# Cross-attention and ternary FFN on one core: the tanh of the weights kept as 16-bit integers and cast by a GpSimd DMA, the output product moved ahead of the token transposes, the artanh series split

## The chip, the cores and the metric

The kernel runs on one core of one Trainium2 chip. The metric is the device time of one execution in microseconds (us), the median over several runs. Lower is better. The profile gives times from the first instruction to the last, the span; the time of an execution also holds a little outside the span.

## The reference, cut to what matters

`x` is 8 batches of 256 tokens of width 256, float32. There are two residual blocks:

```python
x = x + xattn(layernorm(x), ctx_512, Wq, Wkv_expand, Wout)   # 16 heads, 64 keys, causal mask
x = x + ffn(layernorm(x), w1, g1, w2, g2, w3, g3)            # hidden width 1024

def ternary_quant(w):
    s = mean(abs(w))
    return round(tanh(w / (s + 1e-8))) * arctanh(s)          # round(tanh) is -1, 0 or 1
def linear_bit(x, w, g):
    xq = act_quant(rmsnorm(x, g))                            # 8-bit steps per token
    return einsum('bsd,od->bso', xq, ternary_quant(w))
ffn = linear_bit(silu(linear_bit(x, w1, g1)) * linear_bit(x, w2, g2), w3, g3)
```

So each of the three 1024 x 256 weights needs one mean, one tanh with rounding, and one artanh of the mean.

## The kernel before, in words

All instructions are written out by hand, one program for each engine, and the engines meet at counting semaphores. An engine runs its program strictly in order: an instruction that waits holds up everything behind it on that engine. A batch has TB = 2 tiles of 128 tokens.

**Attention, and the front of the FFN, by batch.** Each engine has a function `iteration(j)`, called for j = 0 or 1 to 6, with batch 7 and the FFN's start written out behind it. Iteration j works on several batches at once, so that the engines have work of different stages:

- PE: `scores(j+1)`, the probability transposes `probs_T(j, 0)`, `tokens_T(j-3)` (transposes of the quantised tokens), `project(j-1)` (the output product with `woutT`, L576), `probs_T(j, 1)`, `query(j+2)`, `weigh(j)`, the mask of batch j+2, `recip_T(j)`.
- ACT (from L822): `recip_T_copy(j-1)`, `quantise(j-3)` (L806), `recip_widen(j)`, `probs_T_copy(j, 0)`, `tokens_T_copy(j-3)`, `exponentials(j+1, 0)`, `probs_T_copy(j, 1)`, `exponentials(j+1, 1)`, and last `query_copy(j+2)` (L746), on which the next iteration's `scores` wait.
- DVE (from L1070): `sums(j)` (L972), `divide(j-1)`, two `maximum(j+1, .)`, `shift(j+1, 0)`, `residual(j-1)` (L986, waits for `project`), `shift(j+1, 1)` (L965, waits for the transposes `probs_T(j, 1)` to have read the old probabilities), then `measure_sum`, `token_max(j-2)`, `aggregate_sum`, `centre(j-1)` and `token_recip(j-2)` (L1044) for the FFN's front.
- POOL (from L439): `token_scale(j-3)` (L421, waits for `token_recip`, and `quantise` waits for it), `values(j)`, `factor(j-2)`, `keys(j+2)` (L337, waits until `scores(j+1)` are done), `scaled(j-2)` (L430, waits for `quantise`), `half_sums(j+1)` (L398, on which `sums(j+1)` of DVE waits).

**The weights.** ACT sums absolute values (L774). A matmul adds them over partitions, `weight_scales` (L1098) makes the means `w_s` and `w_inv`. `weight_tanh(i)` (L781) writes tanh as float32 over `w_in`, in place, and `ternary(i)` (L991) rounds it on DVE by adding and subtracting 1.5 * 2^23, with bf16 output into `wT`. ACT calls `weight_tanh(0)` ahead of `recip_widen(2)`, `weight_tanh(1)` behind iteration 3 and `weight_tanh(2)` behind iteration 4; DVE calls the three `ternary` behind its iterations 3, 4 and 5. PE waits for all three before its first up product. The artanh of the three means is computed on POOL, a series for small means (`arctanh_terms`, L373, between iterations 1 and 2) and a logarithm for others (`log_branch`, L385, between iterations 3 and 4). The Ln itself is one small ACT instruction (L868) between `query_copy(4)` and iteration 3; its function is in another table than Exp, so an ACT_TABLE_LOAD stands before it and another before the next Exp.

**The FFN, by tile of 128 tokens.** `schedule(slot)` runs 16 tiles in slots: two up products, Silu, the gate product on DVE, the maximum for the quantisation, the quantised hidden tile `q_h` (int16) transposed by a DMA from SP, a cast on DVE, and the down product. `q_h` is first written in slot 1, long after attention's iterations.

Of the kernel before, what the change touches and what calls it, by code (L numbers as in the profile page):

```python
# [21 lines left out]
ALU = mybir.AluOpType  # L22
ACT = mybir.ActivationFunctionType
# [20 lines left out]
def build_program(nc, x_d, xT_d, ctxT_d, wqT_d, wkvT_d, woutT_d, w1T_d, g1_d, w2T_d, g2_d, w3T_d, g3_d, out_d):  # L44
# [17 lines left out]
    with stack:  # L62
        def sb(name, shape, dt=fp32):
            return stack.enter_context(nc.sbuf_tensor(name, shape, dt))
# [4 lines left out]
        def sem(name):  # L69
            return stack.enter_context(nc.semaphore(name))  # L70
# [72 lines left out]
        abs_done, wsum_done, ws_ready, small_ready, inv_step, inv_ready = map(sem, (  # L143
            "abs_done", "wsum_done", "ws_ready", "small_ready", "inv_step", "inv_ready"))
        ln_in, ln_out, ath_steps, ath_ready = map(sem, ("ln_in", "ln_out", "ath_steps", "ath_ready"))
        tanh_ready, tern_ready = sem("tanh_ready"), sem("tern_ready")

        AHEAD = 6

# [47 lines left out]
        q_h = sb("q_h", [P, 2, H], i16)  # L197
        hT_raw = sb("hT_raw", [P, 2, HC, P], i16)
        hT = sb("hT", [P, 2, HC, P], bf16)
        q_last = probs  # L200
        hT_last = half_sum[:].rearrange("p t n k -> p (t n k)").bitcast(bf16).rearrange("p (t n k) -> p t n k", t=2, k=P)
        y = sb("y", [P, 2, D])
# [45 lines left out]
        with nc.Block() as block:  # L248
# [45 lines left out]
            def _(pool):  # L294
# [71 lines left out]
                def step(instruction):  # L366
                    ath_step[0] += 1
                    instruction.then_inc(ath_steps, 1)
                    pool.wait_ge(ath_steps, ath_step[0])

                sq, poly, log, diff = (w_tmp[:, n, :] for n in range(4))

                def arctanh_terms():  # L373

                    pool.wait_ge(ws_ready, 1)
                    step(g.tensor_scalar(w_ln[:, 0, :], w_s[:], 1.0, None, ALU.add))
                    g.tensor_scalar(w_ln[:, 1, :], w_s[:], -1.0, 1.0, ALU.mult, ALU.add).then_inc(ln_in, 1)
                    step(g.tensor_tensor(out=sq, in0=w_s[:], in1=w_s[:], op=ALU.mult))
                    step(g.tensor_scalar(poly, sq, 2.0 / 13, 2.0 / 11, ALU.mult, ALU.add))
                    for n in (9, 7, 5, 3, 1):  # L380
                        step(g.tensor_tensor(out=poly, in0=poly, in1=sq, op=ALU.mult))
                        step(g.tensor_scalar(poly, poly, 2.0 / n, None, ALU.add))
                    step(g.tensor_tensor(out=poly, in0=poly, in1=w_s[:], op=ALU.mult))

                def log_branch():  # L385

# [52 lines left out]
                def iteration(j):  # L439
                    if from_(j, 3):  # L440
                        token_scale(j - 3)
                    if from_(j, 1):
                        values(j)
                    if from_(j, 2):
                        factor(j - 2)
                    if live(j + 2):
                        keys(j + 2)
                    if from_(j, 2):
                        scaled(j - 2)
                    if live(j + 1):  # L450
                        half_sums(j + 1)

# [33 lines left out]
                pool.wait_ge(v_set, 4)  # L486
                pool.wait_ge(g_ld, 48)
                iteration(1)
                arctanh_terms()
                iteration(2)  # L490
                iteration(3)
                log_branch()
                for j in range(4, B - 1):
                    iteration(j)
                token_scale(4)
                values(7)
# [7 lines left out]
            def _(pe):  # L504
# [130 lines left out]
                def iteration(j):  # L635
                    if live(j + 1):
                        scores(j + 1)
                    if j == 0:
                        pe.wait_ge(v_set, 2)
                    probs_T(j, 0)  # L640
                    if j == 0:
                        values_of(6, bank5)
                    if from_(j, 3):
                        need(pe, rT_ready, j)
                        tokens_T(j - 3, bank5)
                    if from_(j, 1):
                        project(j - 1)
                    probs_T(j, 1)
                    if j == 0:
                        pe.wait_ge(v_set, 4)  # L650
                    if from_(j, 3):
                        need(pe, xqT_ready, j - 2)
                    if live(j + 2):
                        query(j + 2)
                    if j == 1:
                        weight_sum()
                        pe.wait_ge(ws_ready, 1)
                    weigh(j)
                    if live(j + 2):
                        mask(j + 2)  # L660
                    recip_T(j)
# [4 lines left out]
                iteration(1)  # L666
                for j in range(2, B - 1):
                    iteration(j)
                pe.wait_ge(tern_ready, 3)

                def xqT_cols(T, n):

# [70 lines left out]
            def _(act):  # L743
# [37 lines left out]
                def weight_tanh(i):  # L781


                    a.activation(w_in[:, bass.ds(i * WN, WN)], w_in[:, bass.ds(i * WN, WN)], ACT.Tanh,
                                 scale=w_inv[:, bass.ds(i, 1)]).then_inc(tanh_ready, 1)


# [34 lines left out]
                def iteration(j):  # L822
                    if from_(j, 2):
                        recip_T_copy(j - 1)
                    if from_(j, 3):
                        quantise(j - 3)
                    recip_widen(j)
                    probs_T_copy(j, 0)
                    if from_(j, 3):
                        tokens_T_copy(j - 3, bank5)  # L830
                    if live(j + 1):
                        exponentials(j + 1, 0)
                    probs_T_copy(j, 1)
                    if live(j + 1):
                        exponentials(j + 1, 1)
                    if live(j + 2):
                        query_copy(j + 2)
# [17 lines left out]
                exponentials(2, 1)  # L855
                query_copy(3)
                recip_T_copy(1)
                act.wait_ge(inv_ready, 1)
                weight_tanh(0)
                recip_widen(2)  # L860
                probs_T_copy(2, 0)
                act.wait_ge(rstd_done, 4)
# [1 line left out]
                probs_T_copy(2, 1)  # L864
                exponentials(3, 1)
                query_copy(4)
                act.wait_ge(ln_in, 1)
                a.activation(w_ln[:], w_ln[:], ACT.Ln).then_inc(ln_out, 1)  # L868
                iteration(3)
                weight_tanh(1)  # L870
                iteration(4)
                weight_tanh(2)
                iteration(5)


                def silu(T, t, b):
# [59 lines left out]
            def _(dve):  # L936
# [51 lines left out]
                    cols = bass.ds(b * BD, BD)  # L988
                    v.tensor_tensor(x_sb[:, cols], bank4[:], x_sb[:, cols], ALU.add).then_inc(bank4_free, 1)

                def ternary(i):  # L991
                    need(dve, tanh_ready, i + 1)
                    v.tensor_scalar(wT[:, i * WN:(i + 1) * WN], w_in[:, i * WN:(i + 1) * WN],
                                    ROUND, ROUND, ALU.add, ALU.subtract).then_inc(tern_ready, 1)

                dve.wait_ge(ident_set, 1)
                v.tensor_copy(ident_h[:], ident[:]).then_inc(cast_set, 1)
                dve.wait_ge(const_set, 3)
# [110 lines left out]
                for b in (3, 4):  # L1109
                    measure(b)  # L1110
                    aggregate(b)
                sums(0)
                maximum(1, 0)
                maximum(1, 1)
                shift(1, 0)
                shift(1, 1)
                for b in range(5, B):
                    measure(b)
                    aggregate(b)
                iteration(1)  # L1120
                iteration(2)
                iteration(3)
                ternary(0)
                iteration(4)
                ternary(1)
                iteration(5)
                ternary(2)
                dve.wait_ge(w_down_ready, 2)
                dequant(0, 4)
                iteration(6)  # L1130
# [159 lines left out]
```

## Time and profile before

| | us |
|---|---|
| median of 3 runs | 202.84 (201.66 to 203.04) |
| the profiled execution, its own time | 202.36 |
| its span | 200.6 |
| outside the span (202.36 - 200.6) | 1.8 |
| busy: DVE, PE, ACT, POOL | 164.4, 148.5, 142.9, 130.0 |
| mean granted TensorE clock, share of full speed | 0.903 |

Busy time is the union of an engine's instructions. A row of the timeline gives start, duration, engine, line, operation, output and input, and in square brackets the engine's idle time before it with the instruction that ended it. "<-issue" means that nothing in the profile ended that idle time.

### The profile page before, as it was taken

How to read it: one execution, taken by the hardware profiler on the slowest of the kernel's cores; microseconds unless marked ns; L12 is line 12 of the kernel's file. 1: busy time of each engine (PE TensorE's matmuls, PEld its weight loads, DVE VectorE, ACT ScalarE, POOL GpSimd, SP SyncE). 2: the span in 40 equal slices, each digit the busy share in tenths (PEclk: the TensorE clock that was granted, in tenths of full speed). 3: DMA queues.
4: the chain of work that ended last, by engine and by line, in shares of the span. 5: the costliest groups of instructions: out<-in, count | busy, mean ns of one | idle time of the engine just before them, and what ended most of it. 6: DMA issues, size and time to landing. Idle time of an engine off the chain costs nothing.

```text
span 200.6 us, 3287 instructions
## 1 busy us (share of the span) xinstructions
PE 148.5 (74%) x1082; PEld 97.3 (49%) x1082; DVE 164.4 (82%) x309; ACT 142.9 (71%) x195; POOL 130.0 (65%) x212
## 2 busy tenths in 40 slices
PE   5979886888779499697789764284888778775380
PEld 5567655676566377475557341131353243332360
DVE  1179799999788947999959598985989999999950
ACT  2026978985699586895769976696799998896220
POOL 4063727279885883877625669879878988997100
PEclk9999999999969958999699998557699999999588
DMA  5999920000000000000000000220234635534311
GB/s 167 320 379 423 400 117 0 7 0 0 3 2 0 3 0 0 3 0 0 0 3 2 0 0 0 52 52 5 52 80 88 149 82 115 120 78 100 83 54 54
DMA packets 20944, 15.02 MB, mean 75 GB/s; under 512 B 15296, under 2 KB 19648, under 8 KB 20416
## 3 DMA queue, kind: packets, MB, share of 16 engines
q1 hardware_dynamic: 20704, 14.42, 24.9%
q10 hardware_dynamic: 224, 0.39, 0.6%
q8 instruction: 9, 0.15, 0.3%
q14 instruction: 7, 0.06, 0.1%
HBM read 9.04 MB, written 2.10 MB: 56 GB/s over the span
## 4 chain that ended last, share of the span: by engine, by line
DVE 41%; POOL 15%; ACT 14%; PE 14%; issue 12%; DMA 2%; DVEq 0%; POOLq 0%; ACTq 0%
DVE c_max L1160 7%; DVE hh L1136 7%; ACT q_x L812 5%; ACT probs L769 4%; POOL u L434 4%; DVE u_max L1041 4%; PE bank L580 3%; POOL half_sum L404 3%; DVE hT L1147 3%; DVE row_max L962 3%; DVE y L1187 3%; DVE row_sum L975 2%; ACT probsT L754 2%; PE wide L587 2%; DMA out<-y 2%
## 5 line engine op out<-in xcount | busy, mean ns | idle before, releaser
L685 PE MATMUL wide<-wT,xqT 128*128 128x512 bf16 x128 | 36.0, 428 | 7.9 <-DVE hh L1136 6.7
L456 POOL TENSOR_TENSOR c_h<-hh,g3b 128x1024 f32<-128x1024 f32 x15 | 35.4, 2361 | 3.4 <-DVE hh L1136 3.3
L404 POOL TENSOR_TENSOR half_sum<-probs 128x512 f32<-128x512 f32 x16 | 20.3, 1270 | 24.9 <-ACT probs L769 24.9
L685 PEld LDWEIGHTS wide<-wT,xqT 128*128 128x128 bf16 x128 | 12.7, 107 | 25.8 <-issue 9.5
L705 PE MATMUL bank<-wT,hT 128*128 128x256 bf16 x112 | 15.9, 289 | 10.4 <-DVE hT L1147 10.4
L580 PE MATMUL bank<-woutT,attnT 128*128 128x256 f32 x64 | 20.0, 466 | 4.2 <-DVE attnT L983 4.2
L885 ACT ACTIVATE sq_junk<-hh,root_x 128x1024 bf16<-128x1024 f32 x16 | 18.3, 1147 | 5.3 <-DVE hh L1136 4.6
L769 ACT ACTIVATE probs<-probs,ln_rstd 128x1024 f32<-128x1024 f32 x16 | 18.4, 1152 | 4.9 <-DVE probs L968 4.8
L812 ACT ACTIVATE q_x<-u,round_c,qs_x 128x256 f32<-128x256 f32 x32 | 16.6, 588 | 7.1 <-issue 3.6
L434 POOL TENSOR_TENSOR u<-xc,g 128x512 f32<-128x512 f32 x16 | 20.0, 1272 | 2.4 <-ACT q_x L812 2.4
L968 DVE TENSOR_TENSOR probs<-wide,row_max 128x1024 f32<-128x1024 f32 x16 | 19.3, 1217 | 1.7 <-PE bank L506 1.6
L892 ACT ACTIVATE q_h<-c_h,qs_h 128x1024 int16<-128x1024 f32 x14 | 16.1, 1146 | 5.8 <-DVE qs_h L1174 5.8
L754 ACT COPY probsT<-bank 128x512 f32<-128x512 f32 x32 | 17.1, 584 | 3.9 <-PE bank L506 3.9
L962 DVE TENSOR_REDUCE row_max<-wide 128x16 f32<-128x1024 f32 x16 | 18.7, 1210 | 1.3 <-PE wide L540 1.3
L1136 DVE TENSOR_TENSOR hh<-gate,wide 128x1024 f32<-128x1024 f32 x16 | 19.4, 1210 | 0.1
L1160 DVE TENSOR_REDUCE c_max<-c_h 128x1 f32<-128x1024 f32 x16 | 19.3, 1208 | 0.0
L705 PEld LDWEIGHTS bank<-wT,hT 128*128 128x128 bf16 x112 | 10.6, 103 | 17.2 <-DVE hT L1147 15.7
L506 PE MATMUL bank<-ident,probs 128*128 128x128 f32 x128 | 17.8, 284 | 1.2 <-ACT probsT L754 1.2
L580 PEld LDWEIGHTS bank<-woutT,attnT 128*128 128x128 f32 x64 | 14.5, 239 | 7.6 <-DVE attnT L983 5.4
L879 ACT ACTIVATE gate<-wide,dq_x 128x1024 f32<-128x1024 f32 x16 | 17.6, 1100 | 0.0
L506 PEld LDWEIGHTS bank<-ident,probs 128*128 128x128 f32 x128 | 15.1, 147 | 3.8 <-issue 2.1
L521 PE MATMUL bank<-xT,wqT 128*128 128x256 f32 x64 | 15.4, 384 | 0.0
(122 smaller groups left out, 303.3 us busy)
## 6 DMA issues: line engine op xcount, KB each, us to landing
out<-y SPq DMA_DIRECT2D x16, 128.0 KB, 2.0
x_sb<-in_x SPq DMA_DIRECT2D x1, 1280.0 KB, 10.3
xT<-in_xT SPq DMA_DIRECT2D x1, 1280.0 KB, 17.5
w_in<-in_w1T SPq DMA_DIRECT2D x1, 1024.0 KB, 12.3
w_in<-in_w2T SPq DMA_DIRECT2D x1, 1024.0 KB, 11.4
w_in<-in_w3T SPq DMA_DIRECT2D x1, 1024.0 KB, 13.5
x_sb<-in_x SPq DMA_DIRECT2D x1, 512.0 KB, 6.4
xT<-in_xT SPq DMA_DIRECT2D x1, 512.0 KB, 7.2
```

The source lines that it names most:

```text
L404: last = g.tensor_tensor(out=half_sum[:, t, :, :], in0=e[:, :, 0, :], in1=e[:, :, 1, :], op=ALU.add)
L434: last = g.tensor_tensor(out=u[:, t, :, :], in0=xc[:, t, :].unsqueeze(1).to_broadcast([P, 2, D]), in1=g12[:], op=ALU.mult)
L456: g.tensor_tensor(out=c_h[:, t, :], in0=hh[:, t, :], in1=g3b[:], op=ALU.mult).then_inc(c_ready, 1)
L506: return nc.tensor.matmul(out, in_, ident[0:n, 0:n], is_transpose=True, start=True, stop=True)
L580: last = nc.tensor.matmul(bank4[:, t * D:(t + 1) * D], attnT[:, c, t * P:(t + 1) * P], woutT[:, c, :], start=(c == 0), stop=(c == DC - 1))
L685: last = nc.tensor.matmul(wide[:, (w * 2 + n) * 512:(w * 2 + n + 1) * 512], xqT_cols(T, w * DC + c), w_cols[:, c, n * 512:(n + 1) * 512], ...
L705: last = nc.tensor.matmul(down_banks[t][:, 0:D], (hT if T < LAST else hT_last)[:, t, n, :], wT[:, 2 * WN + n * D:2 * WN + (n + 1) * D], st ...
L769: a.activation(probs[:, t, :], probs[:, t, :], ACT.Exp, scale=ln_rstd[:, bass.ds(2 * b + t, 1)]).then_inc(probs_ready, 1)
L812: last = a.activation(q_x[:, t, w, :], u[:, t, w, :], ACT.Identity, scale=qs_x[:, t, w:w + 1], bias=round_c[:, 0:1])
L962: v.tensor_reduce(out=by_pair(row_max[:, t, :]), in_=by_head(wide, t), op=ALU.max, axis=AX.X).then_inc(max_ready, 1)
L1136: v.tensor_tensor(hh[:, t, :], gate[:, t, :], wide[:, H:2 * H], ALU.mult).then_inc(hh_ready, 1)
L1160: v.tensor_reduce(out=c_max[:, t:t + 1], in_=c_h[:, t, :], op=ALU.max, axis=AX.X, apply_absolute_value=True).then_inc(cm_ready, 1)
```

## The change

Five edits:

1. PE: `project(j-1)` goes ahead of `tokens_T(j-3)`; both keep their waits.
2. ACT: `weight_tanh(i)` writes int16 (the conversion rounds) into `tern`, a view of the tile `q_h`, and there is one such buffer: `weight_tanh(1)` and `weight_tanh(2)` wait until the DMA of the one before has landed. The three calls move to iterations 3, 4 and 5, behind `recip_T_copy(j-1)` and ahead of `quantise(j-3)`.
3. POOL: `ternary(i)` is now a DMA issued from GpSimd, `tern` (int16) to `wT` (bf16), in iteration i + 4 between `keys` and `scaled`. The three DVE instructions go. PE waits for all three DMAs.
4. POOL and ACT: the artanh series is cut in two pieces, in iterations 2 and 3 behind `scaled`, and `log_branch` goes into iteration 4 between `scaled` and `half_sums`. The Ln on ACT goes ahead of `recip_widen(2)`, where `weight_tanh(0)` was.
5. DVE: `sums(0)` goes behind the two `maximum(1, .)`.

```diff
@@ POOL
-                def arctanh_terms():
+                def log_inputs():
                     pool.wait_ge(ws_ready, 1)
                     step(g.tensor_scalar(w_ln[:, 0, :], w_s[:], 1.0, None, ALU.add))
                     g.tensor_scalar(w_ln[:, 1, :], w_s[:], -1.0, 1.0, ALU.mult, ALU.add).then_inc(ln_in, 1)
                     step(g.tensor_tensor(out=sq, in0=w_s[:], in1=w_s[:], op=ALU.mult))
-                    step(g.tensor_scalar(poly, sq, 2.0 / 13, 2.0 / 11, ALU.mult, ALU.add))
-                    for n in (9, 7, 5, 3, 1):
+
+                def series(terms):
+                    for n in terms:
+                        if n == 11:
+                            step(g.tensor_scalar(poly, sq, 2.0 / 13, 2.0 / 11, ALU.mult, ALU.add))
+                            continue
                         step(g.tensor_tensor(out=poly, in0=poly, in1=sq, op=ALU.mult))
                         step(g.tensor_scalar(poly, poly, 2.0 / n, None, ALU.add))
-                    step(g.tensor_tensor(out=poly, in0=poly, in1=w_s[:], op=ALU.mult))
+                        if n == 1:
+                            step(g.tensor_tensor(out=poly, in0=poly, in1=w_s[:], op=ALU.mult))
+
+                def ternary(i):
+                    need(pool, tanh_ready, i + 1)
+                    g.dma_start(wT[:, i * WN:(i + 1) * WN], tern).then_inc(tern_ready[i], 16)
...
                     if live(j + 2):
                         keys(j + 2)
+                    if 0 <= j - 4 < 3:
+                        ternary(j - 4)
                     if from_(j, 2):
                         scaled(j - 2)
+                    if j == 2:
+                        series((11, 9, 7, 5))
+                    if j == 3:
+                        series((3, 1))
+                    if j == 4:
+                        log_branch()
                     if live(j + 1):
                         half_sums(j + 1)
...
                 iteration(1)
-                arctanh_terms()
-                iteration(2)
-                iteration(3)
-                log_branch()
-                for j in range(4, B - 1):
+                log_inputs()
+                for j in range(2, B - 1):
                     iteration(j)
@@ PE
+                    if from_(j, 1):
+                        project(j - 1)
                     if from_(j, 3):
                         need(pe, rT_ready, j)
                         tokens_T(j - 3, bank5)
-                    if from_(j, 1):
-                        project(j - 1)
...
-                pe.wait_ge(tern_ready, 3)
+                for i in range(3):
+                    pe.wait_ge(tern_ready[i], 16)
@@ ACT
                 def weight_tanh(i):
-                    a.activation(w_in[:, bass.ds(i * WN, WN)], w_in[:, bass.ds(i * WN, WN)], ACT.Tanh,
+                    if i > 0:
+                        act.wait_ge(tern_ready[i - 1], 16)
+                    a.activation(tern, w_in[:, bass.ds(i * WN, WN)], ACT.Tanh,
                                  scale=w_inv[:, bass.ds(i, 1)]).then_inc(tanh_ready, 1)
...
                     if from_(j, 2):
                         recip_T_copy(j - 1)
+                    if 0 <= j - 3 < 3:
+                        weight_tanh(j - 3)
                     if from_(j, 3):
                         quantise(j - 3)
...
-                act.wait_ge(inv_ready, 1)
-                weight_tanh(0)
+                act.wait_ge(ln_in, 1)
+                a.activation(w_ln[:], w_ln[:], ACT.Ln).then_inc(ln_out, 1)
                 recip_widen(2)
...
-                act.wait_ge(ln_in, 1)
-                a.activation(w_ln[:], w_ln[:], ACT.Ln).then_inc(ln_out, 1)
-                iteration(3)
-                weight_tanh(1)
-                iteration(4)
-                weight_tanh(2)
-                iteration(5)
+                act.wait_ge(inv_ready, 1)
+                for j in range(3, B - 2):
+                    iteration(j)
@@ DVE
-                def ternary(i):
-                    need(dve, tanh_ready, i + 1)
-                    v.tensor_scalar(wT[:, i * WN:(i + 1) * WN], w_in[:, i * WN:(i + 1) * WN],
-                                    ROUND, ROUND, ALU.add, ALU.subtract).then_inc(tern_ready, 1)
...
-                sums(0)
                 maximum(1, 0)
                 maximum(1, 1)
+                sums(0)
...
-                iteration(3)
-                ternary(0)
-                iteration(4)
-                ternary(1)
-                iteration(5)
-                ternary(2)
+                for j in range(1, B - 2):
+                    iteration(j)
```

## Rows read from the trace of the kernel before

**Rows 1.** The page, part 1: busy us (share of the span) xinstructions of each engine
```profile
PE 148.5 (74%) x1082; PEld 97.3 (49%) x1082; DVE 164.4 (82%) x309; ACT 142.9 (71%) x195; POOL 130.0 (65%) x212
```

**Rows 2.** Windows: length, busy of PE, PEld, DVE, ACT, POOL, clock, DMA share, GB/s
```profile
66.70:82.20 15.50, 12.30 (x99) 9.49 (x98) 11.48 (x19) 10.78 (x16) 10.02 (x18) 0.78 0.00 0
82.20:95.20 13.00, 10.00 (x101) 7.43 (x99) 12.54 (x23) 9.59 (x16) 10.20 (x17) 1.00 0.00 1
...
148.00:189.00 41.00, 28.73 (x160) 13.91 (x159) 40.12 (x74) 34.05 (x42) 32.88 (x43) 0.96 0.44 97
```

**Rows 3.** Timeline of DVE, iterations 2 to 5
```profile
51.20 1.22 DVE L1041 TENSOR_REDUCE u_max<-u 128x4 f32<-128x1024 f32 x1 [1.36 <-POOL u L434]
...
65.56 0.17 DVE L1047 RECIPROCAL rm_x<-u_max 128x4 f32<-128x4 f32 x1
...
75.19 0.69 DVE L989 TENSOR_TENSOR x_sb<-bank,x_sb 128x512 f32<-128x512 f32 x1 [2.91 <-PE bank L580]
76.89 1.23 DVE L968 TENSOR_TENSOR probs<-wide,row_max 128x1024 f32<-128x1024 f32 x1 [1.00 <-PE bank L506]
...
80.97 0.16 DVE L1047 RECIPROCAL rm_x<-u_max 128x4 f32<-128x4 f32 x1
81.06 1.19 DVE L993 TENSOR_SCALAR wT<-w_in 128x2048 bf16<-128x2048 f32 x1
...
88.33 1.23 DVE L968 TENSOR_TENSOR probs<-wide,row_max 128x1024 f32<-128x1024 f32 x1
```

**Rows 4.** Timeline of ACT, from the end of iteration 2 into iteration 4
```profile
59.42 1.28 ACT L769 ACT_TABLE_LOAD   x1
...
63.76 0.58 ACT L749 COPY qT<-bank 128x512 f32<-128x512 f32 x1
64.23 2.02 ACT L784 ACTIVATE w_in<-w_in,w_inv 128x2048 f32<-128x2048 f32 x1
...
68.90 2.07 ACT L812 ACTIVATE q_x<-u,round_c,qs_x 128x256 f32<-128x256 f32 x4 [2.18 <-issue]
...
71.38 1.05 ACT L754 COPY probsT<-bank 128x512 f32<-128x512 f32 x2
```

**Rows 5.** Timeline of POOL, iterations 4 and 5
```profile
65.18 0.25 POOL L389 TENSOR_TENSOR w_tmp<-w_ln 128x3 f32<-128x3 f32 x1
...
68.19 0.62 POOL L427 TENSOR_SCALAR qs_x<-rm_x,fb_bound 128x2 f32<-128x2 f32 x2
...
70.85 0.61 POOL L340 TENSOR_TENSOR k_pair<-kT,half_of 128x256 f32<-128x256 f32 x1
71.42 2.49 POOL L434 TENSOR_TENSOR u<-xc,g 128x512 f32<-128x512 f32 x2
...
81.24 1.46 POOL L427 TENSOR_SCALAR qs_x<-rm_x,fb_bound 128x2 f32<-128x2 f32 x2 [0.60 <-DVE rm_x L1047]
```

**Rows 6.** Timeline of PE, iteration 4
```profile
65.05 1.17 PE L540 MATMUL wide<-k_pair,qT 32*128 32x128 f32 x32
66.15 1.09 PE L506 MATMUL bank<-ident,probs 128*128 128x128 f32 x8
...
71.43 3.73 PE L580 MATMUL bank<-woutT,attnT 128*128 128x256 f32 x8
74.95 1.80 PE L506 MATMUL bank<-ident,probs 128*128 128x128 f32 x8
```

**Rows 7.** DMA view: GB/s by 40th of the span; issues, KB each, us to landing
```profile
GB/s 167 320 379 423 400 117 0 7 0 0 3 2 0 3 0 0 3 0 0 0 3 2 0 0 0 52 52 5 52 80 88 149 82 115 120 78 100 83 54 54
...
out<-y SPq DMA_DIRECT2D x16, 128.0 KB, 2.0
...
x_sb<-in_x SPq DMA_DIRECT2D x1, 512.0 KB, 6.4
```

**Rows 8.** The page, part 5: half sums (busy, mean ns, idle before them)
```profile
L404 POOL TENSOR_TENSOR half_sum<-probs 128x512 f32<-128x512 f32 x16 | 20.3, 1270 | 24.9 <-ACT probs L769 24.9
```

**Rows 9.** Timeline of DVE, the start of attention
```profile
22.28 1.22 DVE L975 TENSOR_REDUCE row_sum<-half_sum 128x32 f32<-128x1024 f32 x1 [1.19 <-POOL half_sum L404]
```

More of the change, by code:

```diff
@@ L145, in build_program @@
         ln_in, ln_out, ath_steps, ath_ready = map(sem, ("ln_in", "ln_out", "ath_steps", "ath_ready"))
-        tanh_ready, tern_ready = sem("tanh_ready"), sem("tern_ready")
+        tanh_ready = sem("tanh_ready")
+        tern_ready = [sem(f"tern{i}_ready") for i in (1, 2, 3)]
         AHEAD = 6
@@ L199, in build_program @@
         hT = sb("hT", [P, 2, HC, P], bf16)
+        tern = q_h[:].rearrange("p t n -> p (t n)")
         q_last = probs
@@ L1119, in _ @@
                     aggregate(b)
-                iteration(1)
-                iteration(2)
-                iteration(3)
-                ternary(0)
-                iteration(4)
-                ternary(1)
-                iteration(5)
-                ternary(2)
+                for j in range(1, B - 2):
+                    iteration(j)
                 dve.wait_ge(w_down_ready, 2)
```

## Prediction, made blind

> **What bounds the kernel now.** I read the page first. DVE is the busiest engine, 164.4 us of 200.6, and no engine is full over the whole span [rows 1]. The windows then divide the span. From 148 to 189 us, in the FFN's slots, DVE works 40.12 us of 41.00 [rows 2]: there the end moves only if the start of the slots moves, since the change takes nothing out of them. So the change must pay in the iterations ahead of them. There an iteration with no long stall takes 13.0 us, with DVE busy 12.54 (iteration 5), and one with a stall 15.5 us (iteration 4) [rows 2]. The timelines tell what the stall is. In iteration 4 DVE waits 2.91 us for `project` (the release of L989) and 1.00 us for the transposes `probs_T(4, 1)` ahead of the second `shift` [rows 3]. PE runs `project(3)` only at 71.43, because `tokens_T(1)` stands ahead of it and waits for `quantise(1)`; and it runs it in 3.73 us at a window clock of 0.78 [rows 2, 6]. ACT begins `quantise(1)` at 68.90 after 2.18 us of idle time, since POOL comes to `token_scale(1)` only at 68.19, behind the log branch that began at 65.18 [rows 4, 5].
>
> So there is one loop over engines that sets an iteration: `token_recip` on DVE, `token_scale` on POOL, `quantise` and the copies on ACT, `probs_T(j, 1)` on PE, the second `shift` on DVE, and again to `token_recip`. I measure everything against it. From the end of `rm_x` to the start of the second `shift` it is 76.89 - 65.73 = 11.2 us in iteration 4 and 88.33 - 81.13 = 7.2 us in iteration 5 [rows 3]; the second is DVE's own work, the 1.1 us of a `ternary` in it.
>
> **What the new wait does.** `weight_tanh(1)` stands at the head of ACT's iteration 4 and waits until the DMA of `ternary(0)` has landed. POOL issues that DMA in its own iteration 4, behind `token_scale(1)`, `values`, `factor` and `keys(6)`. `keys(6)` waits for `scores(5)`, and these wait for `query_copy(5)`, ACT's last instruction of iteration 3. So POOL can't issue early: from the end of that copy ACT must wait at least for scores 1.17 [rows 6], keys 0.61 [rows 5] and the DMA, and it can only do `recip_T_copy(3)` meanwhile. Behind the waiting tanh stand `quantise`, `recip_widen`, the copies and the exponentials, so PE's token transposes and `probs_T(4, 1)`, and DVE's second `shift`, wait as well. The same happens in iteration 5. In iteration 3 the tanh has nothing to wait for, and the third DMA has nobody waiting on ACT; PE wants it only at the first up product.
>
> Price of the DMA, issue to landing: no row has a DMA issued by GpSimd, nor one that casts. It moves 128 x 2048 int16, 512 KB. The nearest rows are the stores, 128 KB in 2.0 us, and the load of 512 KB, 6.4 us beside other loads [rows 7]. I take the store, 384 KB more at the best rate seen, 423 GB/s, 0.9 us [rows 7], and 0.6 us for POOL's part: 3.5 us, between 2.0 and 6.4. How long POOL itself is held by the issue no row shows: between nothing and the 2.49 us of its longest piece of work here [rows 5]; I keep it at the 0.6.
>
> The Trainium skill (DMA: Bandwidth & Descriptors, "Anatomy of one DMA — SWDGE (gpsimd) path") gives about 2.0 us plus bytes at 436 GB/s, 3.2 us here; by it the sum below would be 0.6 us less. No run shown here has such a DMA.
>
> The new way from `rm_x` to the second `shift`: 0.1 to `token_scale`; from its start to the end of `keys` 71.46 - 68.19 = 3.3 [rows 5]; DMA 3.5; tanh 2.0; from the start of `quantise` to the end of the copies `probsT` 72.43 - 68.90 = 3.5 [rows 4]; transposes 1.09 [rows 6], of which 0.3 lies beside the second copy. That is 13.2 us, where DVE would be ready after 6.1 (7.2 less a ternary). So DVE idles about 7 us in each of two iterations.
>
> - Iteration 4: 13.2 - 11.2 = +2.0. The wait for `project` goes (it now needs only `attnT`) and so do the `ternary` and the log branch ahead of `token_scale`; all are inside the 11.2.
> - Iteration 5: 13.2 - 7.2 = +6.0.
> - Iteration 6: the third `ternary` goes and no tanh is late: -1.1 (1.19 less the overlap of neighbours) [rows 3]. Its `project` waits for `attnT` in any order, so the swap gives nothing there.
> - The log branch, 3.0 us (65.18 to 68.19) [rows 5], now stands in iteration 4 between `scaled(2)` and the half sums. `quantise(1)` begins 8.9 us after `rm_x` and ends at 11.0; `scaled` 2.5 [rows 5], log 3.0 and two half sums of 1.27 [rows 8] end at 19.0. DVE wants `sums(5)` at 13.2 + 4.2 = 17.4 (4.2 is the way from second `shift` to the end of `rm_x`, 76.89 to 81.13 [rows 3]). +1.6; between 0 and 3.0.
> - The series' split takes POOL's small steps from ahead of `scaled(0)`, so the wait of 1.36 us for `u` in iteration 2 goes [rows 3]; Ln and the return to Exp stand where ACT waits for `shift(3, 0)`, so the 1.28 us load ahead of the exponentials of iteration 3 goes [rows 4]. -2.7; between 0 and -3.5. `weight_tanh(0)` then fills ACT's wait for `token_scale(0)` and costs nothing; without that cover it would cost 2.0.
> - `sums(0)` behind the maxima: they need not wait 1.19 us for the half sums [rows 9], but the reciprocal comes later. -0.7; between 0 and -1.2.
> - Clock: before its 3.73 us `project` PE had been idle for some us, and the eight transposes behind it took 1.80 instead of 1.09 at the window's 0.78 [rows 2, 6]. With PE idle over 5 us ahead of `tokens_T`, I charge the same 0.7 twice: +1.4; between 0 and +3.4.
>
> Sum: 2.0 + 6.0 - 1.1 + 1.6 - 2.7 - 0.7 + 1.4 = +6.5. The profiled execution took 202.36 (span 200.6 and 1.8 around it), 0.5 below the median of the runs; it would take 208.9, and on the median, 202.84, it is 209.3.
>
> One rule speaks for an edit here, and it decides 0.8 us. `token_scale(2)` took 1.46 us where the one before took 0.62 [rows 5], beside `ternary(1)` at 81.06 [rows 3]. With the ternaries gone I count 0.6 in both iterations; were the 1.46 of another cause, iteration 5 would be 0.8 longer. The Trainium skill (SBUF — State Buffer, "Who interferes with whom") says that a DVE instruction in a two-port mode holds the interface shared with GpSimd for its whole length, and also keeps GpSimd from writing DMA descriptors; the trace's 1.46 agrees. By the second half the short `centre` instructions could hold up an issue, but at the issue DVE is in its maxima.
>
> **Rivals.**
> - *The wait is covered, and the kernel gets faster.* For it: POOL idles 24.9 us ahead of its half sums [rows 8], so it might run ahead and issue early. Then iterations 4 and 5 go to 13.0 - 1.1 = 11.9 [rows 2]: -3.6 and -1.1, and with -1.1, -2.7 and -0.7 it is -9.2, 193.6 us. Against it: `keys(6)` ties the issue to ACT's own last copy, shown above. Each us of the DMA counts twice, so from +6.5 at 3.5 us the sum reaches zero at 0.25 us from issue to landing; it decides for the old time below that, and 2.0 is the shortest DMA in the rows.
> - *Loss and gains cancel* (within 1%): a DMA of up to 1.3 us, or gains of 4 us more than I count. 203 us.
> - *Quick landing*, 2.0 to 2.5 us: +3.5 to +4.5, about 206.8.
> - *Slow cast or descriptors*, 5.5 to 6.4 us: +10.5 to +12.3, about 214.5. For it: the 423 GB/s were moved without a cast.
> - *The clock stays low over all of iterations 4 and 5*, with queries and products at double length and on the path: 3.4 on top, 212.7. For it the 3.73 us of `project`; against it the wait of PE for ACT hides most of it.
>
> **How the numbers follow.** The forecast has 0.52; quick landing 0.14, slow DMA 0.15, low clock 0.09; cancelled 0.05; covered 0.05. The time is that of the forecast, 209.3. The range takes the DMA at 2.0 with somewhat better gains at one end, 205.0, and the slow DMA at the other, 214.5; about 0.15 is left out. Faster by over 1% is the covered case, 0.05; within 1%, about what a measurement of this kernel can tell from no change, 0.05; slower 0.90.
>
> **What would show it.** Right: ACT idle 5 to 7 us ahead of the second and of the third tanh, released by the DMA; DVE idle 6 to 7 us ahead of the second `shift` in iterations 4 and 5, released by PE, and none ahead of L989; each of the two iterations about 18 us; FFN slots as before, only later; no L993. Wrong: the two tanh beginning at once, or a landing in under 1.3 us. If the idle time is there but the total isn't, the steps of iterations 2 and 3 were mis-sized.

## The result, and the profile after

The changed kernel takes 208.06 us (median of 4 runs, 206.80 to 211.83), the kernel before 202.55 in the same comparison. The ratio is 1.0257, 95% interval 1.0177 to 1.0337: slower by 2.6%. The medians differ by 5.5 us, the ratio makes it 5.2: an execution more than 1.5% above the fastest of its kernel, here the one of 211.83, is left out of the ratios, in this section and below. The forecast was 209.3, range 205.0 to 214.5. The profiled execution took 206.80 with a span of 205.1; before it was 202.36 and 200.6.

The page's busy time says little: every engine works less than in [rows 1] or as much, and the time is longer.

```profile
PE 145.3 (71%) x1082; PEld 96.0 (47%) x1082; DVE 160.4 (78%) x306; ACT 142.7 (70%) x195; POOL 129.5 (63%) x215
```

The windows are cut where DVE begins a `row_sum`, so they are iterations 4, 5 and 6 with what follows until the first gate product; columns as in [rows 2].

```profile
64.51:82.53 18.02, 11.21 (x88) 8.41 (x80) 10.34 (x18) 10.26 (x15) 10.13 (x20) 0.81 0.08 30
82.53:101.65 19.12, 12.93 (x133) 10.06 (x132) 11.17 (x22) 11.66 (x17) 9.77 (x16) 0.82 0.08 28
101.65:117.10 15.45, 12.26 (x95) 8.78 (x97) 13.33 (x26) 12.89 (x21) 9.38 (x17) 1.00 0.10 36
154.00:195.00 41.00, 28.70 (x160) 13.92 (x159) 39.90 (x74) 33.90 (x42) 32.89 (x43) 0.97 0.44 97
```

Iterations 4 and 5 take 18.0 and 19.1 us against 15.5 and 13.0 in [rows 2], and DVE works 10.3 and 11.2 us in them; the slots of the FFN are as full as before, 39.9 of 41.0. The timeline of ACT shows where the time went in iteration 4, and that of DVE (second fence) who paid.

```profile
62.62 0.60 ACT L768 COPY qT<-bank 128x512 f32<-128x512 f32 x1
64.02 0.59 ACT L784 COPY recipT<-bank 128x512 f32<-128x512 f32 x1 [0.81 <-PE bank L524]
71.02 2.00 ACT L805 ACTIVATE q_h<-w_in,w_inv 128x2048 int16<-128x2048 f32 x1 [6.41 <-DMA wT<-q_h]
72.92 2.06 ACT L833 ACTIVATE q_x<-u,round_c,qs_x 128x256 f32<-128x256 f32 x4
...
88.98 2.00 ACT L805 ACTIVATE q_h<-w_in,w_inv 128x2048 int16<-128x2048 f32 x1 [5.63 <-DMA wT<-q_h]
```

```profile
64.42 0.16 DVE L1061 RECIPROCAL rm_x<-u_max 128x4 f32<-128x4 f32 x1
...
69.93 0.68 DVE L1008 TENSOR_TENSOR x_sb<-bank,x_sb 128x512 f32<-128x512 f32 x1
78.19 1.23 DVE L987 TENSOR_TENSOR probs<-wide,row_max 128x1024 f32<-128x1024 f32 x1 [7.57 <-PE bank L524]
...
96.15 1.23 DVE L987 TENSOR_TENSOR probs<-wide,row_max 128x1024 f32<-128x1024 f32 x1 [7.52 <-PE bank L524]
```

ACT idles 6.41 and 5.63 us and is released by the DMA. DVE idles 7.57 and 7.52 us ahead of the second `shift` of each of the two iterations. The wait of 2.91 us for `project` of [rows 3] is gone. The chain that ended last goes through the DMA itself, in iteration 4 (start, length, what) and again in iteration 5:

```profile
64.50 0.10 DVE rm_x L1061
...
64.69 0.59 POOL qs_x L440 x2
...
67.35 0.52 POOL k_pair L342
67.87 3.13 DMA wT<-q_h
70.99 0.02 issue
71.02 0.04 ACT q_h L805
71.06 1.86 issue
72.92 2.06 ACT q_x L833 x4
...
76.11 1.95 PE bank L524 x8
```

It enters POOL's program at `token_scale` (`qs_x`), which waits for `rm_x`, and not at `scores(5)`, for which `keys(6)` also waits: these had ended 2.2 us before `keys(6)` began.

```profile
63.92 1.17 PE L558 MATMUL wide<-k_pair,qT 32*128 32x128 f32 x32
67.31 0.61 POOL L342 TENSOR_TENSOR k_pair<-kT,half_of 128x256 f32<-128x256 f32 x1
```

And the issues of the DMA view, which no row of before could show:

```profile
wT<-q_h POOLq DMA_DIRECT2D x3, 512.0 KB, 3.0
```

### The profile page after: what moved, and what is told of

Read it like the earlier page. It is cut to its first block, busy times and chain, and to the rows that moved or that the text cites. A ratio compares the mean times of both kernels' runs of the same rounds, so it can differ in the third digit from the quotient of the medians.

```text
span 205.1 us, 3289 instructions
## 1 busy us (share of the span) xinstructions
PE 145.3 (71%) x1082; PEld 96.0 (47%) x1082; DVE 160.4 (78%) x306; ACT 142.7 (70%) x195; POOL 129.5 (63%) x215
## 4 chain that ended last, share of the span: by engine, by line
DVE 44%; ACT 14%; issue 12%; PE 11%; POOL 10%; DMA 6%; DVEq 0%; POOLq 0%; ACTq 0%
DVE c_max L1168 7%; DVE hh L1144 7%; ACT q_x L833 6%; DVE row_max L981 5%; DVE u_max L1055 3%; PE bank L524 3%; POOL u L447 3%; DMA wT<-q_h 3%; DVE probs L987 3%; DVE hT L1155 3%; DVE y L1195 3%; DMA wqT<-in_wqT 3%; ACT probsT L773 3%; DVE row_sum L994 2%; ACT probs L788 2%
## 5 line engine op out<-in xcount | busy, mean ns | idle before, releaser
L704 PE MATMUL wide<-wT,xqT 128*128 128x512 bf16 x128 | 33.7, 407 | 8.3 <-DVE hh L1144 7.1
L724 PE MATMUL bank<-wT,hT 128*128 128x256 bf16 x112 | 16.7, 299 | 12.3 <-DVE hT L1155 12.3
L704 PEld LDWEIGHTS wide<-wT,xqT 128*128 128x128 bf16 x128 | 12.2, 104 | 24.9 <-issue 8.1
L524 PE MATMUL bank<-ident,probs 128*128 128x128 f32 x128 | 18.9, 295 | 2.8 <-ACT probsT L773 2.8
L598 PE MATMUL bank<-woutT,attnT 128*128 128x256 f32 x64 | 15.9, 391 | 5.9 <-DVE attnT L1002 5.9
L724 PEld LDWEIGHTS bank<-wT,hT 128*128 128x128 bf16 x112 | 11.0, 107 | 19.1 <-DVE hT L1155 17.2
L539 PE MATMUL bank<-xT,wqT 128*128 128x256 f32 x64 | 17.1, 414 | 0.3 <-ACT xqT L840 0.3
L636 PE MATMUL bank<-ident_h,q_x 128*128 128x128 bf16 x64 | 6.7, 241 | 13.1 <-ACT q_x L833 13.0
## 6 DMA issues: line engine op xcount, KB each, us to landing
xT<-in_xT SPq DMA_DIRECT2D x1, 1280.0 KB, 17.5
w_in<-in_w3T SPq DMA_DIRECT2D x1, 1024.0 KB, 13.6
```

Source lines behind the costliest of these rows:

```text
L524: return nc.tensor.matmul(out, in_, ident[0:n, 0:n], is_transpose=True, start=True, stop=True)
L704: last = nc.tensor.matmul(wide[:, (w * 2 + n) * 512:(w * 2 + n + 1) * 512], xqT_cols(T, w * DC + c), w_cols[:, c, n * 512:(n + 1) * 512], ...
L724: last = nc.tensor.matmul(down_banks[t][:, 0:D], (hT if T < LAST else hT_last)[:, t, n, :], wT[:, 2 * WN + n * D:2 * WN + (n + 1) * D], st ...
```

## The experiments

The runs were compared with further executions of the kernel before, whose medians lie between 199.4 and 201.8 us; so all comparisons are by ratio to it.

**Three buffers, no wait.** The tanh of each weight gets its own int16 buffer; `hT_raw` and `hT` are as idle there as `q_h`.

```diff
-        tern = q_h[:].rearrange("p t n -> p (t n)")
+        tern = (q_h[:].rearrange("p t n -> p (t n)"), hT_raw[:].rearrange("p t n k -> p (t n k)"),
+                hT[:].rearrange("p t n k -> p (t n k)").bitcast(i16))
...
-                    if i > 0:
-                        act.wait_ge(tern_ready[i - 1], 16)
-                    a.activation(tern, w_in[:, bass.ds(i * WN, WN)], ACT.Tanh,
+                    a.activation(tern[i], w_in[:, bass.ds(i * WN, WN)], ACT.Tanh,
```

> Each tanh writes its own int16 buffer (q_h, hT_raw, hT), so ACT waits for no DMA; all else as in the changed kernel. Theory (the wait for the DMA of the tanh before is the whole loss): both idle stretches of ACT (6.4 and 5.6 us) go, the two waits of DVE ahead of the second shift (7.6 and 7.5 us) shrink to under 1 us, iterations 4 and 5 take about 12 us, and the time is 193 to 197 us, ratio to the kernel before about 0.96. Rival (the loss sits in the moved log branch, the PE order or the GpSimd DMAs as such): the time stays above 203 us.

Measured: 194.67 us, ratio 0.971 (0.963 to 0.979). ACT's row shows the tanh at once, and the DVE windows of iterations 4 and 5 are 11.4 and 12.5 us long.

```profile
63.91 0.59 ACT L785 COPY recipT<-bank 128x512 f32<-128x512 f32 x1 [0.81 <-PE bank L525]
64.39 2.00 ACT L804 ACTIVATE hT_raw<-w_in,w_inv 128x2048 int16<-128x2048 f32 x1
66.29 2.06 ACT L832 ACTIVATE q_x<-u,round_c,qs_x 128x256 f32<-128x256 f32 x4
```

```profile
64.39:75.76 11.37, 9.98 (x112) 7.36 (x108) 11.07 (x18) 10.56 (x17) 10.19 (x20) 1.00 0.13 48
75.76:88.22 12.46, 11.08 (x123) 8.34 (x116) 11.95 (x23) 10.88 (x16) 9.80 (x16) 1.00 0.12 43
88.22:105.40 17.18, 13.50 (x90) 9.52 (x93) 13.48 (x27) 12.95 (x21) 9.40 (x17) 0.90 0.09 32
```

So the wait alone is worth 1.0257 - 0.971 = 5.5%, about 11 us, and all the rest of the change together is a gain. In the two traces the stretch from `sums(2)` to the first gate product shrinks from 75.8 to 65.1 us, by 10.7. The rival that the wait is covered by other work falls.

**One buffer, issued earlier.** POOL issues `ternary(j - 3)` behind `scaled` in iteration j instead of `ternary(j - 4)` behind `keys`.

```diff
-                    if 0 <= j - 4 < 3:
-                        ternary(j - 4)
                     if from_(j, 2):
                         scaled(j - 2)
+                    if 0 <= j - 3 < 3:
+                        ternary(j - 3)
```

> One buffer as in the changed kernel, but POOL issues each DMA one iteration earlier, behind scaled(1), scaled(2) and scaled(3). Theory (not the one buffer but the place of the issue, behind keys, makes ACT wait): the DMA lands about 62.9 us, ahead of the second tanh at 64.6, so there is no wait and the time is that of three buffers within 1%, 193 to 198 us. Rival (a single buffer costs the time anyhow, since tanh, DMA and tanh follow each other): above 202 us.

Measured: 194.15 us, ratio 0.971 (0.966 to 0.976), the same as three buffers. One buffer is enough; it was the place of the issue. POOL's rows of that run:

```profile
59.34 0.79 POOL L396 DMA_DIRECT2D wT<-q_h  x1
70.60 0.65 POOL L396 DMA_DIRECT2D wT<-q_h  x1
81.88 0.66 POOL L396 DMA_DIRECT2D wT<-q_h  x1
```

With 3.0 to 3.1 us the first lands near 62.4, and the second tanh starts at 64.04 without a wait.

**The issue delayed.** Two idle products on POOL ahead of each of the first two issues:

```diff
+                    if i < 2:
+                        flat = g12[:].rearrange("p w d -> p (w d)")
+                        for n in range(2):
+                            g.tensor_tensor(out=c_h[:, n, 0:2 * D], in0=flat, in1=flat, op=ALU.mult)
                     need(pool, tanh_ready, i + 1)
```

> The changed kernel with two extra POOL products of 128 x 512 (1.27 us each, written to an idle tile) ahead of each of the first two DMA issues. Theory (the DMA is on the loop in both iterations, so that each us counts twice): 2.5 us twice, about +5 us on the changed kernel, 212 to 214 us, ratio to the kernel before 1.05. Rival (the loop is closed by something else, with slack at the DMA): below 210 us.

Measured: 210.50 us, ratio 1.054 (1.049 to 1.059). The ratio is as forecast; the time is below the 212 us expected, since the kernel before took only 199.4 in this comparison. The ratio is 0.028 above the changed kernel's, 5.7 us. The two products took 2.04 us and not 2.5, so twice their length is 4.1; with the two intervals (0.5% and 0.8%) that can't be told from 5.7, and the spans of the two profiled executions differ by 4.0. DVE's waits grew by the length of the two products:

```profile
79.72 1.23 DVE L991 TENSOR_TENSOR probs<-wide,row_max 128x1024 f32<-128x1024 f32 x1 [9.58 <-PE bank L528]
...
99.67 1.22 DVE L991 TENSOR_TENSOR probs<-wide,row_max 128x1024 f32<-128x1024 f32 x1 [9.52 <-PE bank L528]
```

9.58 and 9.52 against 7.57 and 7.52, +2.0 each, and both iterations are 2.0 us longer: a us ahead of the landing counts twice.

**All edits but the DMA.** The tanh is float32 in place at its new place on ACT; DVE rounds behind its iterations 3, 4 and 5.

```diff
-                    if i > 0:
-                        act.wait_ge(tern_ready[i - 1], 16)
-                    a.activation(tern, w_in[:, bass.ds(i * WN, WN)], ACT.Tanh,
+                    a.activation(w_in[:, bass.ds(i * WN, WN)], w_in[:, bass.ds(i * WN, WN)], ACT.Tanh,
...
+                    v.tensor_scalar(wT[:, i * WN:(i + 1) * WN], w_in[:, i * WN:(i + 1) * WN],
+                                    ROUND, ROUND, ALU.add, ALU.subtract).then_inc(tern_ready, 1)
...
+                    if j >= 3:
+                        ternary(j - 3)
```

> All edits but the DMA: tanh stays float32 in place at its new place on ACT, DVE rounds behind its iterations 3, 4 and 5. Theory: no wait on ACT, three roundings of 1.1 us back on DVE: 2 to 4 us above the kernel with own buffers, 196 to 200 us. Rival (the three DVE roundings lie in DVE's idle time and cost nothing): equal to the kernel with own buffers within 1%.

Measured: 197.15 us, ratio 0.986 (0.981 to 0.991), 1.5% or 3.1 us above three buffers, as the theory had it. From `sums(2)` to the first gate product the traces have 66.8 us against 65.1, 1.7 of the 3.1. The DMA, when nobody waits for it, is worth about what three roundings of DVE cost; the other four edits are worth 1.4% without it. The same two runs settle the rule on `token_scale`. POOL's rows, first with the roundings on DVE, then with the DMA:

```profile
64.63 1.46 POOL L435 TENSOR_SCALAR qs_x<-rm_x,fb_bound 128x2 f32<-128x2 f32 x2 [0.60 <-DVE rm_x L1056]
76.34 1.50 POOL L435 TENSOR_SCALAR qs_x<-rm_x,fb_bound 128x2 f32<-128x2 f32 x2 [0.61 <-DVE rm_x L1056]
```

```profile
64.57 0.58 POOL L441 TENSOR_SCALAR qs_x<-rm_x,fb_bound 128x2 f32<-128x2 f32 x2 [0.60 <-DVE rm_x L1060]
75.94 0.62 POOL L441 TENSOR_SCALAR qs_x<-rm_x,fb_bound 128x2 f32<-128x2 f32 x2 [0.34 <-DVE rm_x L1060]
```

**The remaining edits**, alone or in one group, on the kernel before. First the PE order only (`project(j - 1)` ahead of `tokens_T(j - 3)`):

```diff
+                    if from_(j, 1):
+                        project(j - 1)
...
-                    if from_(j, 1):
-                        project(j - 1)
```

> The kernel before with only the output product ahead of the token transposes. Theory: DVE's wait of 2.91 us for project in iteration 4 goes and project runs without an idle PE ahead of it, 2 to 4 us faster than before, ratio 0.98 to 0.99. Rival (the wait ahead of the second shift grows by as much, since probs_T(4, 1) waits for quantise and its copies anyway): no change, ratio within 0.5% of 1.

Measured: ratio 0.986 (0.976 to 0.995), inside the forecast, but the size of the gain is not shown. The ratio rests on two of six executions; the medians of all are 200.69 and 200.94 us. In the profiled execution, one of the other four, the 2.91 us wait for `project` is gone and the one ahead of the second `shift` is as before, 0.95 us for 1.00, so iteration 4 is 2.2 us shorter. But DVE now waits for the half sums ahead of `sums(4)`, and iterations 3 and 6 are 1.2 us longer each: `sums(2)` to the first gate product takes 69.7 us against 69.3.

```profile
67.90 1.22 DVE L975 TENSOR_REDUCE row_sum<-half_sum 128x32 f32<-128x1024 f32 x1 [1.17 <-POOL half_sum L404]
```

Then the POOL and ACT moves only: series in two pieces, log branch in iteration 4, Ln and the three tanh at their new places, rounding on DVE:

```diff
+                    if j == 2:
+                        series((11, 9, 7, 5))
+                    if j == 3:
+                        series((3, 1))
+                    if j == 4:
+                        log_branch()
...
-                arctanh_terms()
-                iteration(2)
-                iteration(3)
-                log_branch()
-                for j in range(4, B - 1):
+                log_inputs()
+                for j in range(2, B - 1):
...
+                    if 0 <= j - 3 < 3:
+                        weight_tanh(j - 3)
```

> The kernel before with only the series in two pieces, the log branch in iteration 4, the Ln ahead of recip_widen(2) and the tanh at the head of ACT's iterations 3 to 5 (float32 in place, rounded on DVE). Theory: 2.7 us less in iterations 2 and 3, as predicted, and something in iteration 4, ratio 0.98 to 0.987. Rival (each of these moves only changes which wait stands there): ratio within 0.5% of 1.

Measured: ratio 0.990 (0.982 to 0.998), a smaller gain than the theory's 0.98 to 0.987 and more than the rival's. The same 2.91 us wait is gone here too, with `token_scale(1)` no longer behind the log branch, and the stretch from `sums(2)` to the first gate product is 66.7 us, as with the PE order added (66.8, all edits but the DMA). So the two edits remove one and the same wait, and in these traces the PE order adds nothing to the moves as long as ACT does not wait. Last `sums(0)` behind the maxima only:

```diff
-                sums(0)
...
+                sums(0)
```

> The kernel before with only sums(0) behind the two maxima of batch 1. Theory: 0.7 us less, ratio 0.9965, iteration 1 starts earlier by that. Rival: the later reciprocal takes it back, ratio 1.

Measured: ratio 0.9955 (0.991 to 1.000), as forecast, but the interval touches 1. The rows are clearer: from the first `row_max` to `sums(2)` it takes 26.3 us (14.09 to 40.41) against 27.2 before (14.62 to 41.80).

**The PE order undone in the changed kernel** (tokens ahead of the product again), the first of these diffs backwards:

> The changed kernel with the token transposes ahead of the output product again. Theory: in iterations 4 and 5 project starts only behind quantise and stands ahead of probs_T(j, 1), 2 to 3.7 us longer in each (3.7 at the low clock), ratio to the kernel before 1.045 to 1.06 instead of 1.026. Rival (DVE's second shift waits for ACT's copies, not for PE): ratio 1.02 to 1.035.

Measured: 209.65 us, ratio 1.0455 (1.038 to 1.053), 2.0% above the changed kernel. Iterations 4 and 5 are 1.9 and 2.3 us longer. `project` now waits for the late tokens, and DVE waits for it in both iterations:

```profile
78.04 0.69 DVE L1008 TENSOR_TENSOR x_sb<-bank,x_sb 128x512 f32<-128x512 f32 x1 [9.19 <-PE bank L598]
...
97.88 0.69 DVE L1008 TENSOR_TENSOR x_sb<-bank,x_sb 128x512 f32<-128x512 f32 x1 [9.14 <-PE bank L598]
```

So the swap pays where `quantise` is late: here it gives back 2%, where without the wait no trace shows a gain of it.

**Versions that beat both kernels.** The profile after shows one more wait in iteration 2, on ACT ahead of the exponentials of batch 3, and then on DVE ahead of `sums(3)`:

```profile
46.97 1.28 ACT L788 ACT_TABLE_LOAD   x1 [2.39 <-DVE probs L987]
48.26 1.15 ACT L788 ACTIVATE probs<-probs,ln_rstd 128x1024 f32<-128x1024 f32 x1
```

```profile
52.80 1.22 DVE L994 TENSOR_REDUCE row_sum<-half_sum 128x32 f32<-128x1024 f32 x1 [1.25 <-POOL half_sum L417]
```

The table load for Exp begins only after 2.39 us of idle time, when `shift(3, 0)` has come. Three runs side by side: early issue again; the same with a tiny Exp right behind the Ln; and that with eight products more, to keep PE busy ahead of `project(5)`.

```diff
                 a.activation(w_ln[:], w_ln[:], ACT.Ln).then_inc(ln_out, 1)
+                a.activation(sq_junk[:, 0, 0:1], round_c[:, 1:2], ACT.Exp)
...
+                    if j == B - 2:
+                        need(pe, rT_ready, j)
+                        for _ in range(8):
+                            nc.tensor.matmul(bank5[:, 0:P], ones[:], ones[:], start=True, stop=True)
                     if from_(j, 1):
                         project(j - 1)
```

> The kernel with the DMAs issued one iteration earlier once more, as the base of the two beside it on this chip: ratio 0.966 to 0.976 as in its first run.

Measured: 194.38 us, ratio 0.9645 (0.957 to 0.972), a little below the 0.966 expected; the intervals of its two comparisons overlap.

> Early issue, plus one tiny Exp on ACT right behind the Ln (one column, to an idle tile), so that the Exp table is loaded in ACT's idle time ahead of shift(3, 0). Theory (the load of 1.28 us starts only when the exponential's own wait has ended, and so stands on the loop): DVE's wait of 1.25 us ahead of sums(3) goes, 1.0 to 1.3 us less than early issue, ratio to the kernel before about 0.965. Rival (the load was hidden, as my prediction had it): the same as early issue, and the wait ahead of sums(3) stays.

Measured: 192.50 us, ratio 0.9545 (0.947 to 0.962). The load now lies in idle time, the exponential waits only for DVE, and the wait ahead of `sums(3)` is gone:

```profile
42.53 1.28 ACT L883 ACT_TABLE_LOAD   x1
43.83 0.20 ACT L883 ACTIVATE sq_junk<-round_c 128x1 bf16<-128x1 f32 x1
46.44 1.15 ACT L788 ACTIVATE probs<-probs,ln_rstd 128x1024 f32<-128x1024 f32 x1 [0.93 <-DVE probs L988]
```

From `sums(2)` to `sums(4)` it takes 22.2 us (40.81 to 63.02) against 23.5 (40.49 to 63.97) in the run beside it, 1.3 less. The ratio moved by 1.0%, inside both intervals' reach; the mechanism and its size are shown by the rows alone. The spans of the two profiled executions hide it, 191.2 us with the tiny Exp and 190.7 without: `project(5)` and what follows ran at a lower clock in the first (granted 0.71 in 88.70:91.50), and DVE waited 1.18 us for them.

> The kernel with the tiny Exp, plus eight float32 products of 128 x 128 into an idle bank ahead of project(5), where PE is idle for 1.9 us. Theory (an idle PE is granted the lower clock, and project(5) takes 3.3 us instead of 2.0 for it): project(5) back at 2.0, about 1.3 us less, ratio to the kernel before about 0.959. Rival (the lower clock there follows from something else): project(5) stays above 3 us and the time is unchanged or up to 1 us longer.

Measured: 191.53 us, ratio 0.954 (0.949 to 0.959), equal to the one without. `project(5)` took 1.99 us in it, but so it did without any extra product in the second execution of early issue, the last of these rows; the first row is its first execution, the second the kernel with the tiny Exp alone:

```profile
90.10 3.65 PE L598 MATMUL bank<-woutT,attnT 128*128 128x256 f32 x8 [1.90 <-DVE attnT L1002]
```

```profile
88.75 2.73 PE L598 MATMUL bank<-woutT,attnT 128*128 128x256 f32 x8 [1.90 <-DVE attnT L1003]
```

```profile
89.71 1.99 PE L598 MATMUL bank<-woutT,attnT 128*128 128x256 f32 x8 [1.90 <-DVE attnT L1002]
```

The same 1.90 us of idle PE ahead, three lengths. So whether the extra products keep the clock stays open; only a repeated profile of each could tell. The last two kernels are about 4.5% faster than the kernel before (0.9545 and 0.954).

## Why the prediction was right, point by point

The way and the place were right, and the two large terms, the waits of iterations 4 and 5, held. That the sum came so near was in part luck: the term of iterations 2 and 3 was 2.0 us too good, that of the half sums did not come at all, and the two misses nearly cancel.

The forecast counts an iteration from one `rm_x` to the next, so the traces are cut there too, at the ends of `rm_x`: before 65.73, 81.13, 92.74 and 108.40, after 64.58, 82.60, 100.41 and 114.38. `sums(2)` starts at 41.80 and 41.36, the first gate product at 111.14 and 117.13, the first `row_max` at 14.62 and 15.03. One execution of each:

| part | predicted | measured |
|---|---|---|
| up to the first `row_max` (loads) | 0 | +0.41 |
| to `sums(2)`; `sums(0)` moved | -0.7 | -0.85 |
| iterations 2 and 3 | -2.7 | -0.71 |
| iteration 4 (+2.0 wait, +0.7 clock) | +2.7 | +2.62 |
| iteration 5 (+6.0 wait, +0.7 clock, +1.6 half sums) | +8.3 | +6.20 |
| iteration 6 (third rounding) | -1.1 | -1.69 |
| to the first gate product | 0 | +0.01 |
| FFN | 0 | -1.49 |
| sum | +6.5 | +4.50 |

- **The loop that ties ACT to its own DMA** held as it was priced, but not by the tie that the prediction names. It says that `query_copy(5)` and `scores(5)` hold back `keys(6)`. They would have, but POOL came to `keys(6)` only at 67.31, 2.2 us after `scores(5)`, because `token_scale`, `values` and `factor` stand ahead of it and the first waits for `rm_x`. So the loop is tanh, `quantise`, copies, `probs_T`, second `shift`, `rm_x`, `token_scale` to `keys`, DMA, next tanh: the way that the sum went by. This way from `rm_x` to the second `shift` was said to be 13.2 us; it was 78.19 - 64.58 = 13.6 and 96.15 - 82.60 = 13.6. With the 0.7 charged for the clock the forecast had 13.9.
- **The DMA** was taken at 3.5 us, and took 3.0 to 3.1; POOL itself was held 0.64 to 0.79 us by an issue. The Trainium skill's 3.2 us (DMA: Bandwidth & Descriptors, "Anatomy of one DMA — SWDGE (gpsimd) path") was nearer, and this case's trace agrees with it; a cost of the cast does not show.
- **Half sums, +1.6: this term failed.** `sums(5)` starts right behind `rm_x`, at 82.53, with no wait. POOL's half sums end at 82.10, 17.5 us behind the `rm_x` before instead of 19.0: the log branch took 2.0 us instead of 3.0 (77.60 to 79.60), and the DMA was 0.4 shorter. I had taken the 3.0 from a trace in which one small product of the branch stretches to 1.11 us beside a rounding of DVE, and that rounding is gone: the same effect that I had counted for `token_scale` a paragraph further. The sum also counted twice. It let DVE want `sums(5)` at 17.4 us and charged the clock's 0.7 beside it; with the clock DVE comes at 18.1, which leaves 0.9 of the 1.6. It came at 18.0.

```profile
65.77 1.11 POOL L391 TENSOR_TENSOR w_tmp<-w_tmp,w_small 128x3 f32<-128x3 f32 x1
```

```profile
78.13 0.19 POOL L404 TENSOR_TENSOR w_tmp<-w_tmp,w_small 128x3 f32<-128x3 f32 x1
```

- **Iterations 2 and 3, -2.7: this term was mis-sized, it measured -0.7.** The wait of 1.36 us for `u` did go. The load of 1.28 us ahead of the exponentials of iteration 3 went too, but it had cost DVE nothing in these iterations: in the trace before, the half sums behind it end at 65.22, ahead of DVE's `rm_x` at 65.56. And I put the return to Exp into ACT's idle time ahead of `shift(3, 0)`. It does not go there: it waits with its exponential, and a wait of 1.25 us ahead of `sums(3)` comes of it. The run with the tiny Exp took that one back. In it the stretch from `sums(2)` to the end of the `rm_x` of iteration 3 is 22.3 us, against 23.2 in the changed kernel and 23.9 before: -1.65, the most that this edit came to, with 1.0 us of the forecast never there.
- **The clock, +0.7 twice,** held: `probs_T(4, 1)` took 1.95 us behind 5.5 us of idle PE and two short groups of transposes, 0.86 more than the 1.09 of [rows 6]. In the window 74.00:78.10 the granted clock was 0.50, the lower of the two levels (1.2 of 2.4 GHz). The rival of a low clock over all of both iterations fell: `project(3)` and `project(4)` took 1.99 us each.
- **Iteration 6, -1.7:** 1.1 of it is the third rounding. `project(5)` took 1.99 us instead of 3.44 in these two executions, and the second `shift` followed the first 0.5 us sooner.
- **FFN, -1.5** was no part of the change. The trace of before ends with a wait of 2.95 us for the store of an earlier tile, the trace of after with 0.98; one execution each. In the traces of all runs here this stretch takes 87.4 to 89.5 us, so the difference is no larger than that between executions.
- **The covered rival** was priced at 193.6, -9.2. With the wait really gone the gain is 2.9%, 5.8 us. Iterations 4 and 5 came out as priced there, 11.4 and 12.5 together where it said 11.9 twice. What lacked was outside them. From `sums(2)` to `sums(4)` it took 24.1 us instead of 25.0, where the rival priced 3.8 less (the 2.7, and the first rounding). Iteration 6 with what follows took 17.2 us instead of 15.9. There `project(5)` was no longer than before (3.31 and 3.44 us), but the token transposes, 1.01 us, now stand between it and `probs_T(6, 1)`, and DVE waits 1.09 us ahead of its second `shift` instead of 0.28, and 2.36 us for `recipT` instead of 1.79. With `project(5)` at 1.99 us, as in the changed kernel's trace, this wait does not show: so at the low clock the swap has a price in iteration 6, which the prediction put at nothing.
- **Quick landing and slow cast** are settled by the 3.0 us. "Each us counts twice" is confirmed by the delayed issue, +2.0 us of DVE's wait in each of the two iterations for 2.0 us of delay.

## What to carry to other kernels

A buffer reused through an asynchronous copy ties its writer to the place of the copy's issue, not only to its length: follow in both programs what must have happened before the issue, and if the way leads back to the writer's own output, as here over PE, DVE and POOL's program order, the whole way is paid once per reuse. Of several waits that tie the issue, look for the one that ends last. Here the cure was free, an idle tile more or the same issue one stage earlier, and it turned 2.6% slower into 2.9% faster. Where an edit takes an instruction off one engine, price the operations of the others that ran beside it anew. And before an operation that goes away is booked as a gain, look whether the engine that sets the pace waits behind it at all.

## What the runs showed of the hardware that was not expected

- The ACT_TABLE_LOAD did not begin before the semaphore wait of the instruction it serves had ended: 1.28 us of load began after 2.39 us of idle time, and a one-column Exp (0.20 us) put ahead moved it out of the way.
- Very small POOL operations are stretched by a DVE rounding of 128 x 2048 float32 beside them: `token_scale` 1.46 to 1.50 us instead of 0.58 to 0.62, each time that it ran beside the rounding (in iteration 4 of the kernel before it came after it, and took 0.62); one small product of the log branch took 1.11 us in the trace of before, 0.19 in that of after.
- A GpSimd DMA of 512 KB between two SBUF tiles with a cast from int16 to bf16 lands in 3.0 to 3.1 us from issue, in all three issues and in each kernel here that has it.
- The same program was granted different clocks for the same stretch in two executions: `project(5)` 3.65 and 1.99 us behind the same 1.90 us of idle time, with a granted clock of 0.52 (90.00:92.00) in the first and 1.00 (89.50:91.90) in the second.
